# Attention probabilities of two of four batches turned by VectorE blocks and a trip through DRAM instead of by TensorE

## The reference, cut to what matters

```python
x = x + xattn(layernorm(x), ctx, ctx, mask)   # x: (128, 32, 1024), ctx: (128, 257, 256)
x = x + s4(layernorm(x))                      # a convolution of 1024 taps, as products with a Toeplitz strip
x = x + ffn(layernorm(x))                     # 64 experts of rank 8, the top 16 of them gated

def xattn(q, k, v, mask):                     # 32 query heads of 32, 8 groups of 4 heads share a key head
    scores = einsum('bsgrd,btgd->bgrst', q, k) / sqrt(32) + mask
    probs = softmax(scores.astype(float32), axis=-1)
    return einsum('bgrst,btgd->bsgrd', probs, v)
```

## Time and profile before

| | |
|---|---|
| median of 3 runs | 1291.4 us (1287.3 to 1295.49) |
| the profiled execution, device time | 1286.13 us |
| its span, first to last instruction | 1284.3 us |
| TensorE busy (matmuls) | 1238.2 us, 96% |
| ScalarE busy | 1121.2 us, 87% |
| VectorE busy | 976.1 us, 76% |
| GpSimd busy | 827.1 us, 64% |
| DMA moved | 166.38 MB, 130 GB/s on average |
| mean granted TensorE clock | 0.993 of full speed |

### The profile page before, as it was taken

How to read it: one execution, slowest core, us unless ns; L and a number is a source line. 1 busy time by engine, 2 the same in 40 slices (tenths; PEclk the granted TensorE clock), 3 DMA queues, 4 the chain that set the end, 5 groups by cost and what they waited for, 6 DMA issues and landing times.

```text
span 1284.3 us, 41514 instructions
## 1 busy us (share of the span) xinstructions
PE 1238.2 (96%) x13676; PEld 1075.3 (84%) x13676; DVE 976.1 (76%) x3424; ACT 1121.2 (87%) x3337; POOL 827.1 (64%) x1259
## 2 busy tenths in 40 slices
PE   4679999999999999999999999999999999999997
PEld 3568888888888888888888888888888888888886
DVE  7877777877777777777877877778777777777753
ACT  6999999999899989898998989999998999899851
POOL 5477667677666667766767766676776666677420
PEclk9799999999999999999999999999999999999999
DMA  7543444444443444444344444444444434444210
GB/s 246 158 148 114 139 120 137 139 130 139 130 139 109 148 138 123 130 146 125 117 139 155 122 122 147 117 133 139 137 138 123 139 118 139 138 124 127 55 60 33
DMA packets 150103, 166.38 MB, mean 130 GB/s; under 512 B 58217, under 2 KB 116082, under 8 KB 149890
## 3 DMA queue, kind: packets, MB, share of 16 engines
q1 hardware_dynamic: 149890, 163.72, 42.7%
HBM read 128.50 MB, written 34.08 MB: 127 GB/s over the span
## 4 chain that ended last, share of the span: by engine, by line
PE 93%; ACT 2%; DVE 2%; DMA 1%; issue 1%; POOL 0%; SPq 0%; DVEq 0%; ACTq 0%; POOLq 0%
PE ps_p L561 27%; PE ps_p L647 17%; PE ps_p L632 17%; PE ps_p L660 14%; PE ps_p L593 10%; PE ps_s L573 9%; ACT pr L851 1%; DMA tmp<-in_wide 0%; ACT pts L783 0%; DMA qx<-turn_q 0%; DVE ms L1398 0%; DVE x L1254 0%; PE ps_p L519 0%; DMA turn_q<-xq 0%; ACT xq L865 0%
## 5 line engine op out<-in xcount | busy, mean ns | idle before, releaser
L851 ACT ACTIVATE pr<-ms,negmax 128x256 f32<-128x256 f32 x1024 | 513.8, 505 | 1.4 <-DVE negmax L1398 1.3
L1398 DVE CUSTOM_DVE_ANT_0 ms<-ps_s,neg_mask,last 128x256 f32<-128x256 f32 x1024 | 455.2, 473 | 55.4 <-PE ps_s L573 55.1
L783 ACT ACTIVATE pts<-ps_p 128x512 f32<-128x512 f32 x512 | 296.4, 593 | 51.4 <-PE ps_p L561 47.5
L561 PE MATMUL ps_p<-ident,pr 128*128 128x128 f32 x2048 | 305.2, 277 | 9.6 <-ACT pr L851 3.5
L561 PEld LDWEIGHTS ps_p<-ident,pr 128*128 128x128 f32 x2048 | 239.2, 141 | 46.1 <-issue 13.7
L851 ACT ACTIVATION_READ_ACCUMULATOR pr<-ms,negmax 128x1 f32 x1024 | 200.4, 196 | 0.0
L1072 POOL TENSOR_TENSOR kt<-kr,kt 128x512 fp32r<-128x512 f32 x128 | 165.6, 1293 | 29.5 <-ACT kt L783 29.5
L647 PE MATMUL ps_p<-wa_hi,ut_hi 128*128 128x288 f32 x512 | 177.6, 347 | 1.4 <-DVE ut_lo L1214 1.4
L647 PE MATMUL ps_p<-wa_lo,ut_hi 128*128 128x288 f32 x512 | 151.2, 295 | 0.0
L647 PE MATMUL ps_p<-wa_hi,ut_lo 128*128 128x288 f32 x512 | 150.6, 294 | 0.0
L1114 POOL TENSOR_TENSOR lastp<-lastp 128x256 f32<-128x256 f32 (+4 forms) x320 | 129.8, 405 | 22.6
(11 more groups left out here) (139 smaller groups left out, 2562.5 us busy)
## 6 DMA issues: line engine op xcount, KB each, us to landing
cx<-in_ctx SPq DMA_DIRECT2D x128, 256.0 KB, 3.1
kr<-in_keys SPq DMA_DIRECT2D x128, 256.0 KB, 3.7
xq<-in_x SPq DMA_DIRECT2D x32, 512.0 KB, 4.0
turn_q<-xq SPq DMA_DIRECT2D x32, 512.0 KB, 3.7
qx<-turn_q SPq DMA_DIRECT2D x128, 128.0 KB, 2.9
xr<-in_x SPq DMA_DIRECT2D x32, 512.0 KB, 4.3
out_x<-tmp SPq DMA_DIRECT2D x32, 512.0 KB, 5.1
dn<-den SPq DMA_DIRECT2D x512, 2.0 KB, 1.8
```

What stands on the lines that cost most here:

```text
L561: mm = pe.transpose(into[:, j * P:(j + 1) * P], source, ident[:, :])
L783: return act.activation(out, in_, ACT.Copy, scale=scale)
L851: act.activation(pr[:, b % 2, g, :], ms[:, n % MS, :], ACT.Exp, bias=negmax[:, n % MS:n % MS + 1], scale=-1.0, accum_out=den[:, b, g:g + 1 ...
L1398: dve.tensor_tensor_reduce(ms[:, n % MS, :], ps_s[:, g % GPH, g // GPH * SW:(g // GPH + 1) * SW], neg_mask[:, 0:SW], 1.0, last[:, it % 2, ...
```

## The change

Batches 0 and 2 of every tile (`TURNED`) no longer pass through `pair_chunk` and `pair_copy`. Instead:

- `exp` writes a group's 256 probabilities into a half of `pr` (four groups) in eight runs of 32, so that blocks of 32x32 lie in the order in which they are wanted.
- `p_turn` (VectorE, new, four a tile: both halves of batches 0 and 2) transposes such a half in place: 128x1024 float32 in 32x32 blocks.
- `store_p` (SyncE, new, four a tile, one DMA each) writes the half, 512 KB, to the DRAM tensor `turn_p`, in runs of 1 KB.
- `load_p` (SyncE, new, two a tile, four DMAs each) reads a batch, 1 MB, back into four slots of `pts` with the partitions exchanged, in runs of 2 KB.
- `attend` reads a turned batch from `pts` with a moving operand of four runs of 32 columns, 2 KB apart.
- `exp` of the batch that reuses the half of `pr` waits for `store_p` to have landed; `load_p` waits for the `attend` of the other turned batch that used the slots; `pair_copy` waits as the ring now requires.

`BANKS` is dealt out anew, and the order of all five engines is new.

```diff
-PAIRS = STEPS // 2
+TURNED = (0, 2,)
...
+def paired(m):
+    return sum(k // GPH not in TURNED for k in range(m))
+PAIRS = paired(STEPS // 2)
...
+            def store_p(it, k, h):
+                sp.wait_ge(p_turned[k][h], at(it, 1, 1))
+                if at(it, 64, 0) > 0:
+                    sp.wait_ge(p_loaded[k], at(it, 64, 0))
+                sp.dma_start(turn_p[k, :, :, h, :],
+                             pr[:, TURNED[k] % 2, GPH * h:GPH * (h + 1), :]).then_inc(p_stored[k][h], 16)
+
+            def load_p(it, k):
+                b = TURNED[k]
+                for h in range(HALVES):
+                    sp.wait_ge(p_stored[k][h], at(it, 16, 16))
+                if at(it, 2 * BPT, 2 * b - 2) > 0:
+                    sp.wait_ge(pv_done, at(it, 2 * BPT, 2 * b - 2))
+                own = pts[:, b % 2 * GPH:(b % 2 + 1) * GPH, :]
+                for i in range(GPH):
+                    sp.dma_start(own[SEQ * i:SEQ * (i + 1), :, :],
+                                 turn_p[k, :, i, :, :].rearrange("(r t) h c -> t r (h c)", r=REP)).then_inc(p_loaded[k], 16)
...
             def attend(it, hh):
                 b, h = hh // 2, hh % 2
-                pe.wait_ge(pc_done, at(it, PAIRS, 2 * hh + 2))
+                if b in TURNED:
+                    pe.wait_ge(p_loaded[TURNED.index(b)], at(it, 64, 64))
+                else:
+                    pe.wait_ge(pc_done, at(it, PAIRS, paired(2 * hh + 2)))
+                turned = pts[:, b % 2 * GPH:(b % 2 + 1) * GPH, :].rearrange("p r (h j q s) -> p h j q r s", h=HALVES, j=TBLK, q=GPH)
...
+                                       turned[:, h, j, q, :, :] if b in TURNED else
                                        pts[:, (2 * hh + q // 2) % PTS, (2 * (q % 2) + j) * P:(2 * (q % 2) + j + 1) * P],
...
             def exp(it, n):
...
+                if g % GPH == 0 and at(it, BPT, b - 2) >= 0:
+                    tile, before, h = (it, b - 2, g // GPH) if b >= 2 else (it - 1, b + 2, g // GPH)
+                    if before in TURNED:
+                        act.wait_ge(p_stored[TURNED.index(before)][h], at(tile, 16, 16))
+                    else:
+                        act.wait_ge(pt_done, at(tile, PAIRS, paired(4 * before + 2 * h + 2)))
+                out, masked = pr[:, b % 2, g, :], ms[:, n % MS, :]
+                if b in TURNED:
+                    out = pr[:, b % 2, g // GPH * GPH:(g // GPH + 1) * GPH, :].rearrange("p g c -> p (g c)").rearrange(
+                        "p (i j g t) -> p g j i t", i=GPH, j=TBLK, g=GPH)[:, g % GPH, :, :, :]
+                    masked = masked.rearrange("p (j i t) -> p j i t", j=TBLK, i=GPH)
...
+            def p_turn(it, k, h):
+                b = TURNED[k]
+                dve.wait_ge(e_done, at(it, STEPS, GROUPS * b + GPH * (h + 1)))
+                half = pr[:, b % 2, GPH * h:GPH * (h + 1), :].rearrange("p g c -> p (g c)")
+                dve.transpose(half, half).then_inc(p_turned[k][h], 1)
```

More of the change, by code:

```diff
@@ L67 @@
 BANKS = {
[L68 to L71 removed]
+    "pair": (0, 0, 1, 2, 3, 0, 3, 2, 3, 0, 0, 2, 1, 3, 0, 1,),
+    "out": (3, 0,),
+    "u": (0, 3,),
+    "z": (0, 1,),
     "g": (1,),
[L73 to L79 removed]
+    "y": (0, 3,),
+    "f": (1, 2,),
+    "b": (2, 3,),
+    "o": (1, 2, 3, 0,),
+    "keys": (0,),
+    "router": (1,),
+    "sums": (3,),
     "dft": (0,),
[L81 to L83 removed]
+    "rows": (3,),
+    "strip": (1, 0, 2,),
+    "w": (3, 0, 2, 1, 0, 3, 0, 2, 1, 0, 3, 0, 1, 2, 1, 1,),
 }
@@ L754, in _ @@
[L754 to L758 removed]
+            keys_transpose(); weight_chunk(0, 0); router_product(); weight_chunk(0, 1); weight_chunk(1, 0)
@@ L775, in _ @@
-            u_chunk(31, 0); expand(30, 1, 2, 4); u_chunk(31, 1); convolve(31, 0, 0, 4); convolve(31, 1, 0, 8)
-            z_chunk(31, 0, 1); z_chunk(31, 1, 1); experts(31, 1, 0, 8); experts(31, 0, 0, 8); gated_chunk(31)
+            scores(31, 0); pair_chunk(30, 12); experts(29, 1, 0, 1); experts(29, 1, 1, 2); experts(29, 1, 2, 5)
+            pair_chunk(30, 13); pair_chunk(30, 14); pair_chunk(30, 15); scores(31, 1); experts(29, 1, 5, 8)
+            attend(30, 4); attend(30, 5); attend(30, 6); attend(30, 7); experts(29, 0, 0, 2); out_chunk(30, 0)
@@ new lines, in _ @@
+            out_chunk(30, 1); scores(31, 2); pair_chunk(31, 4); experts(29, 0, 2, 3); pair_chunk(31, 5)
+            experts(29, 0, 3, 5); pair_chunk(31, 6); experts(29, 0, 5, 6); experts(29, 0, 6, 8); pair_chunk(31, 7)
+            u_chunk(30, 0); u_chunk(30, 1); scores(31, 3); gated_chunk(29); convolve(30, 0, 0, 4)
+            convolve(30, 1, 0, 1); convolve(30, 1, 1, 8); attend(31, 0); attend(31, 1); expand(29, 0, 0, 3)
+            expand(29, 0, 3, 4); expand(29, 1, 0, 3); expand(29, 1, 3, 4); z_chunk(30, 0, 0); pair_chunk(31, 12)
@@ new lines, in _ @@
+            attend(31, 2); pair_chunk(31, 13); attend(31, 3); pair_chunk(31, 14); z_chunk(30, 1, 0); attend(31, 4)
+            attend(31, 5); attend(31, 6); pair_chunk(31, 15); experts(30, 1, 0, 2); attend(31, 7)
+            experts(30, 1, 2, 4); out_chunk(31, 0); experts(30, 1, 4, 8); out_chunk(31, 1); experts(30, 0, 0, 3)
+            experts(30, 0, 3, 4); experts(30, 0, 4, 8); gated_chunk(30); u_chunk(31, 0); u_chunk(31, 1)
+            expand(30, 0, 0, 4); convolve(31, 0, 0, 4); convolve(31, 1, 0, 8); z_chunk(31, 0, 1); z_chunk(31, 1, 1)
@@ new lines, in _ @@
+            maximum(1, 2); maximum(1, 3); s4_step(); maximum(1, 4); maximum(1, 5); s4_step(); maximum(1, 6)
+            maximum(1, 7); weight_low(6, 0); normalisers(0); p_turn(1, 0, 0); maximum(1, 8); maximum(1, 9)
+            maximum(1, 10); maximum(1, 11); maximum(1, 12); maximum(1, 13); maximum(1, 14); maximum(1, 15)
+            out_half(0, 0); out_half(0, 1); p_turn(1, 0, 1); maximum(1, 16); maximum(1, 17); u_stats(0, 0)
+            u_stats(0, 1); maximum(1, 18); u_stats(0, 2); maximum(1, 19); weight_low(6, 1); strip_low(0)
```

585 lines of the change are left out of this document (270 added, 315 removed).

## The result

Slower, and by much: a median of 1447.8 us (1446.2 to 1452.9, four runs) against 1292.6 before (1287.3 to 1295.5, four runs), a ratio of 1.123 with a 95% interval of 1.120 to 1.126. The forecast was 1256.

A forecast was written before the change was run, and what follows sets the result against it. TensorE, with matmuls in flight for all 37.73 us of an iteration, was taken as the bound. Gains of 29 x 0.98 us, 3 in the head and 4 in the drain made 35 us off 1291.4: 1256 us, range 1218 to 1291.

The forecast's parts named there:

- The transposition: VectorE's `p_turn` of 128x1024: 1.14 us each, between 0.62 and 1.40; four an iteration make 4.6 us.
- the scattered writes of `exp`: ScalarE writing probabilities in runs of 32: costed at nothing, at most 1.6 us an iteration, off the loop.
- TensorE's moving operand in runs of 32: Attends of turned batches: taken as 0, at most 1.01 us on the loop; as a slow-operand rival 1285 us, chance 0.04.
- ahead of `u_chunk`: TensorE was to wait there for `row_norm`, about 2 us an iteration, 1.5 to 2.5 as the sign.
- VectorE and GpSimd did not exclude each other: Rival case: `first_residual` on GpSimd and `p_turn` lock each other out, 1.1 us later, 1279 us, chance 0.03.
- The loop of 36.75 us: Longest closed path through one iteration, over VectorE, GpSimd's scale, `row_norm` and TensorE: new period 36.75 us, 0.98 less than before.
- before and after it: Head and drain outside the steady part: gains of 3 us (ScalarE's chain) and 4 us (TensorE's chunks).
- Its four issues take 2.5 us and land 1.8 later, about 4.5 us into the iteration: `move_den` 3 on SyncE's queue, behind `load_p` and `store`: row sums landed before `normalisers` came up at 5.5 us.
- a slack of 1 us: Margin between row sums landing about 4.5 us into the iteration and `normalisers`, on the loop, at 5.5.
- Nothing as well: Wait of `attend` for a turned batch's store and load: costed at nothing, batch 2 being wanted 18 us after turning.
- The DMA rings fill up: Rival, chance 0.10: 4.2 MB more an iteration delay row sums and keys; period 38.5 to 40, time 1310 to 1350 us.
- the sign: DMA share of an iteration: near 0.8 if the forecast held, above 0.9 if it was wrong.

The follow-up runs named there:

- the thinned run: The changed kernel moving, from tile 1 on, only a quarter of each store and load of probabilities, all steps and waits kept: 1254.4 us.

## Why the prediction was wrong

**What held.** The engines' part. The transposition took 1.16 us against 1.14 assumed; the scattered writes of `exp` cost nothing (499 ns, against 505 before), by the groups of ScalarE's instructions:

```profile
L886 ACT ACTIVATE pr<-ms,negmax 128x256 f32<-128x256 f32 x1024 | 508.9, 499 | 51.1 <-DVE negmax L1420 49.6 <-DMA turn_p<-pr 0.9
```

TensorE's moving operand in runs of 32 cost nothing either: in the thinned run the 32 products of two attends of a turned batch stand in the chain at 1.01 us, as in the earlier trace rows. TensorE waited 1.3 us ahead of `u_chunk` there, where about 2 were predicted. VectorE and GpSimd did not exclude each other: the two products of `first_residual` took 1279 ns each (median) with the transposition beside them, 1291 before. The loop of 36.75 us was measured at 36.37 once three quarters of the bytes were gone. That the run then took 1254.4 us, against 1256 forecast, is partly luck: 29 x (37.73 - 36.37) = 39 us were gained in the steady part instead of 28, and about 3 lost before and after it, where 7 were to be gained.

**The step that failed** is "Its four issues take 2.5 us and land 1.8 later, about 4.5 us into the iteration". The issues took 2.6; the landing took 7.8 there, and 6.4 in the median. The 1.8 was read from a profile in which no `load_p` stood ahead. With a slack of 1 us a landing 4.6 us later leaves 3.6 us of waiting; VectorE waited 5.9 us an iteration (189.2 in 32). The prediction had bytes and rates, but set them against the whole iteration, under the rival of the rings. Set against SyncE's list they would have raised the alarm, though not given the size: 2.36 MB at its 315 GB/s are 7.5 us, and the same division says 5.0 where the runs with 1.57 MB ahead measured 2.3 to 4.2.

"Nothing as well" for `attend` failed beside it. The prediction gave store and load "some 10 us". Batch 2's second store is issued by 617.45, and TensorE starts its attends 17.6 us later; over the run it waited 62.3 us for the loads. SyncE's list alone puts 8 us between that store and the loads, and the last load takes 7.8 to land:

```profile
616.19 1.26 SPq L400 DMA_DIRECT2D turn_p<-pr  x2
635.02 3.27 PE L641 MATMUL ps_p<-pts,cx 128*32 128x128 f32 x64 [2.62 <-DMA pts<-turn_p]
```

The landing of the row sums is the term that was wrong, but mending it by order doesn't bring the time back. Five orders with all the bytes had VectorE wait for row sums only 6.1 to 10.2 us in all, and took 1413.9 to 1496.4 us. The prediction had no term for a transfer on its loop at all; in three of these five another transfer took the place, the output or batch 2's loads, by the chains of waits.

**The rival that was nearest** was *The DMA rings fill up*, at 0.10. Its mechanism, row sums queued behind bytes, is what the runs show, its condition is not. It was to decide "from about 230 GB/s downward" (its own numbers, 4.2 MB in the 19.75 us that the old traffic leaves of 36.75, say 213), for an iteration as a whole, and its time was 1310 to 1350. The rings carried 300 GB/s in the burst and were busy 0.73 of the time, below the 0.9 that I had named as the sign. That the time went past the rival's fits a late landing that is not only waited for once: it stops VectorE, through GpSimd SyncE, and SyncE's next 30 us of issues start late.

**A cost with no term in the sum** is the clock. When TensorE has waited for the maxima, its granted clock falls soon after it is back at work (windows; the column before the last two):

```profile
628.00:634.00 6.00, 3.30 (x42) 2.72 (x40) 2.60 (x9) 5.73 (x17) 2.15 (x5) 1.00 0.93 224
634.00:643.00 9.00, 4.88 (x75) 4.09 (x75) 4.55 (x24) 4.62 (x17) 3.61 (x4) 0.81 0.59 214
643.40:644.50 1.10, 1.08 (x25) 0.97 (x26) 1.10 (x3) 0.15 (x2) 1.10 (x3) 1.00 0.18 57
645.00:647.00 2.00, 2.00 (x11) 2.00 (x10) 2.00 (x5) 1.72 (x7) 1.67 (x2) 0.50 0.05 17
```

TensorE's timeline has the idle ahead of it and the same product before and after:

```profile
628.20 0.29 PE L696 MATMUL ps_p<-wa_hi,ut_lo 128*128 128x288 f32 x1
...
643.42 0.98 PE L617 MATMUL ps_s<-kt,qs 32*128 32x256 f32 x24 [3.53 <-DVE negmax L1420]
...
647.10 0.44 PE L696 MATMUL ps_p<-wa_hi,ut_lo 128*128 128x288 f32 x1
```

TensorE resumes at 643.42 behind 3.5 us without work. At 643.4 to 644.5 us the granted clock is still 1.00, at 645 to 647 it is 0.50, the lower of its two levels (1.2 GHz), and the product takes 0.44 us instead of 0.29. Over the run the clock is 0.933, and 0.981 in the thinned run, whose TensorE is idle for 2.1 us at most in the steady part. How much of the 43 us this is was not tried alone.

**What stays open.** Why the orders with late statistics (1482.6 us) and with late last rows (1496.4 and 1484.3) are slower than the change itself; how much of the 155 us goes through the row sums and how much through the other waits; and whether some order of SyncE's list keeps both trips and stays under the kernel before. Nine orders with all the bytes gave 1391.5 to 1496.4; that is no proof that there is none.

## What to carry to other kernels

A transfer's landing time belongs to the queue in which it was measured. Where a change adds bytes, take the list of issues of the queue and sum the bytes that are asked for in the few microseconds ahead of each small transfer that an engine waits for; a mean share over an iteration says nothing of it (four kernels with the same bytes took 1282 to 1424 us). Bytes over rate only tells whether there is something to fear: it gave 7.9 us for a median of 6.4, and 5.2 for landings of 2.3 to 4.2. The price comes from a kernel that thins the new transfers and keeps every step and wait. And where all engines run in fixed orders with a wait on SyncE among them, moving the one transfer that waits can hand the wait to another: of nine other orders with all the bytes four were slower than the change, and the best was at 1391.5 us.

## What the runs showed of the hardware

- A queue of its own gave the four 2 KB transfers hardly a way past the burst: a median of 6.1 us to landing on ScalarE's queue, where the same four took 6.7 on SyncE's.
- In slices of 0.55 us in which the DMA engines were busy for 90% or more they carried from 142 to 438 GB/s; the burst, which mixes runs of 1 KB and 2 KB with half-megabyte rows, had 300 on average.
- The same 0.79 MB ahead of a small transfer cost 3.8 us as loads of probabilities in runs of 2 KB and 2.1 us as context and residual rows.
- TensorE's granted clock fell to 0.50 about 1 us after it had resumed from 3.5 us without work, and a product of 0.29 us then took 0.44: such a wait costs more than its length.
- Writing `exp`'s result in runs of 32 elements across the row took ScalarE no longer than writing it in one piece.
